# Two preactivation convolutions: the quantized convolution of a step issued before the slot's mixing products

## The reference

```
# layer 0
x = x + conv0(gn(x))      # 3x3, pad 1; gn(x) is quantized to whole numbers in -127..127
                          # with one scale, the maximum of |gn(x)| over the whole batch / 128
# layer 1
x = x + conv1(gn(x))      # rfft2, 3x3 complex convolution over frequencies, pad 1, bias, irfft2

def gn(v):                # 8 groups of 2 channels, over the group's pixels
    return (g - mean) / sqrt(var + 1e-5)
```

## Time and profile before

| | us |
|---|---|
| median of 3 runs | 3472.81 |
| lowest and highest | 3467.41, 3480.56 |
| profiled execution | 3469.19 |
| its span | 3467.5 |
| PE busy | 3194.4 (92%) |
| DVE busy | 2965.4 (86%) |
| ACT busy | 1908.3 (55%) |
| POOL busy | 2004.5 (58%) |
| granted PE clock, mean | 0.962 of full |

### The profile page before, as it was taken

The page is one execution under the profiler, slowest core; times in us unless marked ns, Lnnn a source line. Parts: engine busy times, 40 slices in busy tenths (PEclk is TensorE's granted clock), DMA queues, the critical chain, the costliest instruction groups (busy, mean ns, idle before and its releaser), DMA issues.

```text
span 3467.5 us, 125723 instructions
## 1 busy us (share of the span) xinstructions
PE 3194.4 (92%) x45156; PEld 2630.8 (76%) x45156; DVE 2965.4 (86%) x5369; ACT 1908.3 (55%) x2831; POOL 2004.5 (58%) x2961
## 2 busy tenths in 40 slices
PE   6988884799999999999999999999999999999998
PEld 3544442488888888888888888888888888888888
DVE  7999998688888888888888888888888888888886
ACT  7999996344444444444444444444444444444443
POOL 3777400256666666666666666666666666666654
PEclk8999997799999999999999999999999999999999
DMA  8777763267777777777767777777777777777765
GB/s 309 245 244 243 240 240 99 67 208 213 211 212 211 217 213 221 215 214 218 217 210 217 216 216 211 219 213 213 220 214 212 212 219 215 212 210 216 218 192 179
DMA packets 545362, 735.72 MB, mean 212 GB/s; under 512 B 80272, under 2 KB 485872, under 8 KB 529296
## 3 DMA queue, kind: packets, MB, share of 16 engines
q1 hardware_dynamic: 351248, 467.90, 40.9%
q0 software_dynamic: 46080, 125.89, 13.8%
q10 hardware_dynamic: 147456, 134.28, 13.6%
HBM read 266.07 MB, written 135.79 MB: 116 GB/s over the span
## 4 chain that ended last, share of the span: by engine, by line
PE 52%; DVE 16%; DMA 6%; issue 5%; SPq 3%; POOL 1%; ACT 0%; DVEq 0%; ACTq 0%; POOLq 0%
PE y_ps L1084 15%; PE x_ps L1071 8%; PE conv_ps L1116 7%; PE fin_ps L1103 6%; DMA stack<-xn 6%; PE t_ps L1062 4%; DVE img L916 4%; SPq L513 3%; PE conv_ps L1118 3%; PE fin_ps L1098 2%; DVE y_lo L909 2%; PE mean_b L1127 2%; DVE img L926 2%; DVE xn L903 1%; DVE bn L918 1%
## 5 line engine op out<-in xcount | busy, mean ns | idle before, releaser
L601 ACT ACTIVATE xt<-t_ps 128x512 f32<-128x512 f32 x512 | 305.7, 597 | 999.4 <-PE t_ps L1062 910.2
L1084 PE MATMUL y_ps<-mix_w,stack 128*128 128x64 f16 x24576 | 811.7, 194 | 18.8 <-DMA stack<-xn 18.1
L1084 PEld LDWEIGHTS y_ps<-mix_w,stack 128*128 128x128 f16 x24576 | 792.7, 99 | 36.0 <-DMA stack<-xn 26.6
L794 POOL DMA_DIRECT2D img<-in_x x960 | 530.3, 553 | 462.0 <-DMA out<-img 404.8
L804 POOL TENSOR_SCALAR eo<-img,norm 128x256 f32<-128x256 f32 x512 | 477.9, 933 | 368.2 <-PE t_ps L1062 200.5
L916 DVE SCALAR_TENSOR_TENSOR img<-conv_ps,cst,img 128x512 f32<-128x512 f32 x512 | 383.2, 748 | 221.6 <-PE conv_ps L1118 216.4
L1071 PE MATMUL x_ps<-dft,xt 128*128 128x128 f32 x4096 | 562.1, 282 | 0.0
L1071 PEld LDWEIGHTS x_ps<-dft,xt 128*128 128x128 f32 x4096 | 518.5, 199 | 0.0
L594 ACT ACTIVATE scaled<-img,b,a 128x512 int16<-128x512 f32 x512 | 412.3, 805 | 96.7 <-DMA img<-in_x 40.8
L1103 PE MATMUL fin_ps<-inv,y_hi 128*128 128x128 f16 x4096 | 461.2, 222 | 0.0
L1116 PE MATMUL conv_ps<-quant,conv_w 128*128 128x512 f16 x1536 | 422.1, 384 | 34.8 <-DVE quant L897 25.7
(11 more groups left out here) (146 smaller groups left out, 5187.6 us busy)
## 6 DMA issues: line engine op xcount, KB each, us to landing
stack<-xn SPq DMA_DIRECT2D x2048, 132.0 KB, 3.3
out<-img ACTq DMA_DIRECT2D x1024, 128.0 KB, 3.4
img<-in_x SPq DMA_DIRECT2D x120, 1024.0 KB, 4.9
img<-in_x POOLq DMA_DIRECT2D x960, 128.0 KB, 3.4
halo<-quant SPq DMA_DIRECT2D x192, 193.3 KB, 4.2
halo<-quant SPq DMA_DIRECT2D x64, 169.1 KB, 3.9
img<-in_x SPq DMA_DIRECT2D x64, 128.0 KB, 2.7
kept<-rmx SPq DMA_DIRECT2D x32, 48.0 KB, 4.5
```

What stands on the lines that cost most here:

```text
L794: pool.dma_start(img[u][:, hb, :], src[:, :, hb, :]).then_inc(pair_s[u][j], 16)
L1084: last = nc.tensor.matmul(y_ps[t % 2][:, g, b, :], stack[:, t % 2, g, first:first + F], mix_w[:, 2 * at + b, g, f, part, :], start=i == 0, ...
```

## The change

In PE's `period` the block that issues the convolution and the row sums moves up, ahead of the mix and of the first `group_stat`. Nothing else changes: the same instructions, the same waits, the same buffers, and the other four streams as they were.

```diff
--- before.py
+++ after.py
@@ -1191,10 +1191,6 @@
                         mean_rows(s + 1, i + u, 1 - u)
                     if conv and t == IMAGE_AT + 2:
                         mix_rows(s + 1)
-                    if runs(mix, conv, t + 1):
-                        mix_pair(s, t + 1)
-                    if conv and t == STATS_AT:
-                        group_stat(s + 1, meane_s, 0, gmean_s)
                     d, c = conv_of(t)
                     if conv if d == 1 else ahead:
                         conv_pair(s + d, c)
@@ -1202,6 +1198,10 @@
                             row_means(s + d, m)
                         if d == 1 or c:
                             row_means(s + d, c)
+                    if runs(mix, conv, t + 1):
+                        mix_pair(s, t + 1)
+                    if conv and t == STATS_AT:
+                        group_stat(s + 1, meane_s, 0, gmean_s)
                     if conv and t == STATS_AT:
                         group_stat(s + 1, e_s, 1, gvar_s)
                     if mix:
```

## The result

The changed kernel takes 3553.45 us in the median of 3 runs (3536.05 to 3556.95), the kernel before 3472.81. The ratio is 1.0217, with a 95% interval of 1.0156 to 1.0277: 2.2% slower, some 80 us, where I had forecast 3484 us. The profiled execution took 3556.95 us; its span is 3555.3 us, 87.8 more than before.

A forecast was written before the change was run, and what follows sets the result against it. PE was taken to set the pace of ordinary steps, so only its standing still could change. The terms summed to +13 us on the profiled 3469.19, plus half the 3.6 us gap to the median: 3484 us, range 3440 to 3528.

The forecast's parts named there:

- halo, step 1: Step 1's convolution starts earlier, its halo transfer is issued later; PE stands 1.3 us per sample, +40 us.
- halo, step 5: Same halo wait in step 5, part of the later issue hidden by DVE's late x_low: 0.7 us each, +22 us.
- halo, step 13: Step 13's halo is issued at step 12, with row products between; no loss expected.
- statistics: Once per sample, the earlier convolution ends DVE's wait and DVE starts earlier: 0.96 us times 31, -30 us.
- clock: At the statistics step, PE's changed idle time makes drops of the clock slightly rarer: -8 us.
- row_n: PE's 0.27 us wait for row_n once per sample is covered by DVE's earlier start: -7 us.
- restacked tiles: PE's 18.1 us of waits for restacked tiles shrink, as the waiting mix comes 1.09 us later: -8 us.
- y_lo: PE's 8.3 us of waits for y_lo shrink: -4 us.
- ACT and DVE held up: ACT's y_high, stores and x_high come later, mostly covered by DVE's former wait for the convolution: +8 us.
- rival B: The shorter statistics stall keeps the clock up, a further -29 us: 3455 us, chance 0.10.
- Rival C: ACT becomes the late engine in steps 1 to 4, PE waits for y_lo or x_low: 3528 us, chance 0.22.
- Rivals A: The halo lands in time, shrinking the stalls of steps 1 and 5 from 62 to 19 us: 3441 us, chance 0.18.

The follow-up runs named there:

- run 1: The changed kernel with the mix put back in front of the convolution in steps 1 and 5: 3463.79 us, 0.997 of the kernel before.
- run 2: The kernel before with convolution and row sums ahead of the mix in steps 1 and 5 only: 3520.46 us, ratio 1.0113.
- run 7: The changed kernel with the halo transfers of steps 0 and 4 issued ahead of the previous step's restack: 3471.38 us, 1.0006 of the kernel before.
- Run 3: The kernel before with the convolution ahead of the mix in step 10 (the statistics) only: 3439.29 us, ratio 0.9882.
- run 4: The changed kernel with ACT's two stores issued ahead of y_high: 3516.02 us, 1.0122 of the kernel before.
- run 11: The changed kernel with POOL's three folds per pair cut to 16 of 128 columns, output not the reference's: 3521.10 us, 1.014 of the kernel before.
- run 6: The kernel before with only ACT's stores issued ahead of y_high: 3446.24 us, ratio 0.9916.
- run 10: The kernel before with ACT's stores ahead of y_high and the convolution first in step 10 only: 3411.97 us, ratio 0.9812.

## Why the prediction was wrong, point by point

| term | forecast | measured |
|---|---|---|
| halo, step 1 | +40 | +36 |
| halo, step 5 | +22 | +48 |
| halo, step 13 | 0 | +3 |
| statistics | -30 | -11 as waits of PE; +4 as net distance |
| clock | -8 | +13 |
| row_n | -7 | -7 |
| restacked tiles | -8 | -5 |
| y_lo | -4 | +5.5 |
| ACT and DVE held up | +8 | in the rows for the statistics and y_lo |

The entries are what PE's waits changed by; -11 is L948 and L939 together. The net distance is 31 x 0.14 us, and some waits for y_lo and restacked tiles are part of it.

- **Ordinary steps** stay at 4.72 us: right, shown by the windows.
- **Halo, step 1**: right in mechanism and near in size. Runs 1, 2 and 7 show it: the waits go if the convolution is put back or the transfer issued earlier.
- **Halo, step 5**: the mechanism was right, the size wrong. I let DVE's late x_low hide part of SP's move and took the landing of one sample, 3.7 us. In the sample shown above it is 4.6. The mean over the samples, from the first issue to the last landing, grew from 4.4 to 5.2 us, and the issue came 0.5 us later, counted from PE's transform of step 4. My bounds held it; the value taken lay too near the sample that I happened to look at. Why landing got slower is not shown. The DMA engines are 94% busy between issue and landing before and 96% after.
- **Statistics**: the step of my sum that failed is the gain of 0.96 us, and in it "so it can start some 0.28 us earlier", said of DVE. It assumed that DVE arrives at the step as it did before. It arrives 1.1 us later in the sample shown and 0.5 in the mean, and the forecast of -30 became +4 by the net distance. I had named this as a sign of being wrong: the statistics step is no shorter (net 12.80 and 12.94 us). Run 3 shows the gain where DVE is in time, runs 4 and 11 that the stores in front of L601 and the folds beside L897 take most of it away.
- **Clock**: wrong sign, -8 forecast and +13 measured. My term looked at the statistics step alone, and said of the halo's stalls only, against rival B, that they are PE idle time too. Of the 26 us more at 1.2 GHz, 16 lie away from the statistics, and all but the one at the end of the span begin at the end of a halo wait of 1.9 to 2.6 us. Without the halo waits and with the same order at the statistics the time at 1.2 GHz is 118.9 and 104.1 us (runs 1 and 7), under the 126.8 of before, so the sign would have been right without them. The Trainium skill, "TensorE: Matmul & The Clock Gate", section "HAM oscillation — how this bites in real kernels", tells of a kernel whose TensorE is slowed anew behind each wait for a transfer. The trace agrees in kind for these six waits, and not for the other nine of 1.9 us or more. At the statistics neither the rule nor my reading tells which sample slows: after the earlier trace rows's stall of 2.08 us 23 of 30 do, and after one of 1.5 to 2.2 us in run 4 18 of 30.
- **Rival C** named the place, "y_high, the issue of two stores and the next turn-out follow each other", but priced it as PE waiting for y_lo and x_low. The waits for y_lo are 13.8 us, and ordinary steps did not lengthen. It struck in the statistics step, where DVE is the last to arrive.
- **Rivals A and B** did not come about: the halo entry is 85.9 us, and the clock lost instead of winning.

The median lies 69 us above the forecast and 25 above the range. By PE's waits the miss is step 5's halo (+26), the clock (+21), the statistics (+19) and y_lo (+10). I treated the gains and the losses as independent. Two of them were not: the halo's stalls brought the low clock that I had counted as a gain, and the late mix, by way of ACT's stores, took the gain at the statistics.

## What to carry to other kernels

Whoever moves work ahead of another on one engine should list, for the work that comes later, everything queued behind its consumers on each engine, DMA issues included, and check whether the engine that a gain depends on still arrives as early as in the old trace. Where the slack of a transfer is known from one sample, read it in many before multiplying by their number. Here the order of the mix was not bad in itself: with two small mends in the other streams the same order is 2% faster than before. The stores alone give 0.8% in the old order (run 6), and with the new order in the statistics step alone it is 1.9% (run 10).

## What the runs showed of the hardware

- DVE's rounding (128x512, int16 to f16) takes 0.29 us alone. If it starts in the first of POOL's last two folds (L805) and runs over 0.45 us, it ends 0.16 us behind the second one (L807) in the median of 87 cases. One that started in the fold before them (L804) took 1.99 us. Nothing in the list of waits shows it: the time counts as DVE being busy. Only the mean per instruction (487 and 568 ns against a shortest of 279) gives it away.
- Two DMA issues on ACT hold its stream for 1.27 us when they follow one another behind a late activation. With them put between activations that were waiting anyway, the kernel before gained 0.84%.
- PE's waits of 1.9 to 2.6 us for the halo were followed by a stretch at 1.2 GHz in six of 15 cases in the changed kernel. At the statistics a stall of 2.08 us, with a full convolution in front of it, was followed by one in 23 of 30 samples of the kernel before.
